# First layer of a four-layer transformer kernel: the spread of the head norms goes to the shifted scores' two PSUM banks, inside the MLP, and the splitting behind it among the last maxima

## The chip, the core and the metric

One core of a Trainium2 chip. The metric is device time in microseconds (us) of one execution, taken as the median of 3 runs. Of its engines the text uses these names: PE is TensorE (its matmuls), DVE is VectorE, ACT is ScalarE, POOL is GpSimd, SP is SyncE, which here issues nearly all DMAs of the main loop.

## What is computed

Four transformer layers over 32 sequences of 128 tokens with 144 features and 16 heads of 9 features. Layers 0 to 2 attend over the tokens, layer 3 over the heads of each token. The layers are alike but for this: only the first one normalises queries and keys per head. Cut from the reference:

```python
h = modulate(rmsnorm(x, g1, D), scale_msa, shift_msa)
qkv = h @ qkv_w.T + qkv_b
q = rmsnorm(q, qg, HEAD_DIM)          # layer 0 only
k = rmsnorm(k, kg, HEAD_DIM)          # layer 0 only
attn = softmax(einsum('bhqd,bhkd->bhqk', q * HEAD_DIM ** (-0.5), k))
o = einsum('bhqk,bhkd->bhqd', attn, v) @ proj_w.T + proj_b
x = x + gate_msa * o
h2 = modulate(rmsnorm(x, g2, D), scale_mlp, shift_mlp)
x = x + gate_mlp * (gelu(h2 @ fc1_w.T + fc1_b) @ fc2_w.T + fc2_b)
```

## The kernel before

The work is cut into 32 groups of 4 sequences: groups 0 to 7 are layer 0, 8 to 15 layer 1, and so on. Each engine runs its own written-out program, in order, and semaphores (`need(eng, name, g, k)`) tie them together. There is no scheduler: the order in the code is the order on the engine.

The main loop has one **body** per group g, from -1 to 31, and three groups are in work in it: g itself, J = g + 1 and L = g + 2.

- **Attention of g.** 16 steps. A step i multiplies keys and queries of 4 heads into one of two PSUM banks `st_bank` (`shifted_scores`, L1363), ACT takes the exponential out of it (L777), PE weights the values (L1383). The shift is the row maximum of each head, which is brought into the operand by small DMAs (`load_max`, L441, 2 DMAs for each of the 4 sequences b): step 0 needs sequence 0's (`m_loaded0`), step 4 needs `m_loaded1`, **step 8 needs `m_loaded2`** and step 12 `m_loaded3`.
- **In its gaps, the queries and keys of L** (L1283, L1287), in the other two banks, `score_bank`. In layer 0 DVE copies them out (`raw`), ACT squares them, PE sums them per head (L1295), ACT takes logarithm and exponential (`head_norms`, each with a table load), DVE refines the result (`newton`, its last line L1012).
- **Transition.** `o_to_tokens(g, 3)` (L1391), then in layer 0 `spread_norms(L)` (L1307): three matmuls T = 0, 1, 2 that copy each head's factor to its features, into `score_bank`; DVE multiplies (`fit`, L1021), ACT rounds to bf16 (`high`, L697), DVE takes the rest and rounds it (`mid`, L1030 and L1038), POOL takes what is left (`lows`, L563). PE goes on behind the spread with the values of J, first half (V0, L1317), the projection's second half, V1, and the MLP of g.
- **MLP of g** (`up` L1421, `down` L1447), first half, then second half, and among it the scores of J for their maxima (`scores`, L1338, steps 0 to 11; DVE `maximum`, L1052). At the end the maxima are turned by PE (L1347), copied by ACT (`copy_max`, L732) and loaded by DMA, upon which the next body's attention begins.

SP's order in a body is: maxima of g, sequences 2 and 3; store the 12 pieces of L's split queries and keys (`store_parts`, L390 and L384; 1.7 MB of writes); read them back, ordered for the scores, 4 DMAs of 512 KB (`load_stack`, L400); maxima of J, sequences 0 and 1; wait for g's last residual and load J's gates (L366, 2 DMAs of 288 KB). What is stored in body g for L is first used by `scores(L, 0)`, a body later.

Bodies 0 to 5 are those that have both g in work and a group L of layer 0 (groups 2 to 7).

Of the kernel before, what the change touches and what calls it, by code (L numbers as in the profile page):

```python
# [170 lines left out]
def blocks_kernel(nc, t, out):  # L171

    ctx = ExitStack()
    with ctx:  # L174
# [164 lines left out]
        def _(eng):  # L339
# [110 lines left out]
            def body(g):  # L450
                J, L = g + 1, g + 2
                if g >= 0 and flow_of(g) == "a":
                    load_max(g, 2)
                    load_max(g, 3)
                if J < NG and flow_of(J) == "t":
                    mix_values(J)
                if L < NG:
                    if L == FIRST_TOKEN_GROUP:
                        mask_on(L)
                    store_parts(L)  # L460
                    if L == 1:
                        eng.wait_ge(setup["split"], 7 * LAYERS)
                    load_stack(L)
                if J < NG and flow_of(J) == "a":
                    load_max(J, 0)
                    load_max(J, 1)

                if g < 0:
                    return
                need(eng, "x_mlp", g, 1)  # L470
                if layer_of(g) == LAYERS - 1:
                    at = first_seq(g)
                    eng.dma_start(out[at:at + GB].rearrange("b t d -> t b d"), x[:, at:at + GB, :])\
                       .then_inc(setup["out"], 16)
                if J < NG:
                    load_gates(J)
# [7 lines left out]
        def _(eng):  # L484
# [95 lines left out]
            def body(g):  # L580
# [13 lines left out]
                if L < NG and not layer_of(L):  # L594

                    lows(L)
                if g >= 0:
                    rstd_of(g, 1, 1)
                    add_mlp(g, 0)
                    add_mlp(g, 1)  # L600
# [6 lines left out]
        def _(eng):  # L607
# [196 lines left out]
            def body(g):  # L804
# [10 lines left out]
                if normed_heads:  # L815
                    high(L, 0)
                    high(L, 1)
                if g >= 0:
                    copy_oT(g, 3)
                if normed_heads:  # L820
                    high(L, 2)
                if g >= 0:
                    modulated(g, 1, 0)
                if late:
                    values(J, 1)
                if J < NG and not late:
                    mixed_values(J)
                for h in range(2 if g >= 0 else 0):
# [8 lines left out]
                    if h == 0:  # L837
                        modulated(g, 1, 1)
                if g >= 0:
                    first_use("exp_table", g, ACT.Exp)  # L840
# [9 lines left out]
        def _(eng):  # L850
# [165 lines left out]
            def fit(L):  # L1016

                for T in range(QKT):
                    need(eng, "spread_done", L, T)
                    need(eng, "qk_sq", L, T)  # L1020
                    eng.tensor_tensor(qk_raw[:, T, :], qk_raw[:, T, :], score_bank[T % 2][0:QKM, :], ALU.mult)\  # L1021
# [135 lines left out]
            def body(g):  # L1157
# [35 lines left out]
                if normed_heads:  # L1193
                    normalise(M, 0)
                    fit(L)
                    for T in range(QKT):
                        mid(L, T)
# [10 lines left out]
                if g >= 0:  # L1208
                    last_parts(g, 1, 1)
                    residual(g, 0, 1)  # L1210
                if J < NG:
                    for i in range(2, AHEAD):
                        maximum(J, i)
                        if i % CHUNKS == CHUNKS - 1:
                            split_max(J, i // CHUNKS)
                if g >= 0:
                    residual(g, 1, 1)
# [6 lines left out]
        def _(eng):  # L1224
# [41 lines left out]
            def queries_keys(L, T, long=True, short=True):  # L1266
# [5 lines left out]
                if long:  # L1272
# [3 lines left out]
                    if T < 2:  # L1276

                        need(eng, "max_done", L - 2, STEPS - 2 + T)
                        if L == 1:
                            need(eng, "qk_scaled", 0, QKT - 1)  # L1280
# [18 lines left out]
            def spread_norms(L):  # L1299

                need(eng, "norm_y", L, 0)
                for T in range(QKT):
                    if T == 0:
                        need(eng, "qk_taken", L, 2)
                    if T == 2:
                        need(eng, "qk_scaled", L, 0)
                    eng.matmul(score_bank[T % 2][0:QKM, :], spread[:, T * QKM:(T + 1) * QKM], norm_y[:, 1, :],  # L1307
# [13 lines left out]
            def scores(g, i):  # L1321
# [9 lines left out]
                elif g + 1 < NG:  # L1331

                    name = "qk_taken" if layer_of(g + 1) else "qk_scaled"
                    need(eng, name, g + 1, (2, 1)[i])
# [15 lines left out]
            def shifted_scores(g, i):  # L1350
# [8 lines left out]
                else:  # L1359
                    need(eng, "exp_done", g - 1, i - 2 + STEPS)  # L1360
                for j in range(CH):
# [144 lines left out]
            def body(g):  # L1506
# [6 lines left out]
                if L < NG and layer_of(L) == 0:  # L1513
# [25 lines left out]
                flip_rows(g, 1, 1)  # L1539
                down(g, 0)  # L1540
# [68 lines left out]
```

## Time and profile before

| what | value |
|---|---|
| median of 3 runs | 1935.79 us (1934.92 to 1936.99) |
| the profiled execution, its own time | 1931.41 us |
| its span | 1929.6 us |
| mean granted clock of TensorE | 0.875 of full speed |
| busy | PE 83%, DVE 66%, ACT 48%, POOL 20% of the span |

The profiled execution is 4.4 us shorter than the median. The granted clock has two levels in the rows below, 0.50 (1.2 GHz) and 1.00 (2.4 GHz), and a number between them where a window holds both. Times in rows are us from the start of the span. The first body with attention starts at 150.65 us; layer 0's bodies 0 to 5 fill 150.65 to 557.79 us.

### The profile page before, as it was taken

What the parts mean: (1) busy time and instruction counts of PE and PEld (TensorE: products, weight loads), DVE (VectorE), ACT (ScalarE), POOL (GpSimd) and SP (SyncE); (2) the same over time, 40 slices, a digit from 0 to 9 for tenths busy, and PEclk for the clock granted to TensorE, in tenths of its full rate; (3) what the DMA queues carried; (4) which work ended last, traced back from release to release, by engine and by line L of the source; (5) the groups of instructions that cost most, each with busy time, mean ns of one, the idle gap of its engine ahead of it and who ended that gap; (6) DMA issues with size and microseconds to landing.
All of it is one profiled execution on the core that took longest, in us unless ns stands there. A gap on an engine that the chain in (4) does not pass through costs nothing. (4 is left out here: it accounts for less than half of the span.)

```text
span 1929.6 us, 37580 instructions
## 1 busy us (share of the span) xinstructions
PE 1609.7 (83%) x13794; PEld 1045.1 (54%) x13794; DVE 1265.1 (66%) x3174; ACT 934.0 (48%) x2095; POOL 382.1 (20%) x432
## 2 busy tenths in 40 slices
PE   7357977977888999999898998989878777977888
PEld 4124544554455666666666666656555455555556
DVE  5664666576577767666767767676676677566743
ACT  0124445544555555555555556555444444443544
POOL 1020111011021111111111111111331434143310
PEclk9957777878899999998989989899788789787978
DMA  6150331232144433333333434343675777557530
GB/s 175 49 142 21 95 81 40 69 94 58 38 116 102 100 94 97 95 95 92 97 91 98 97 98 100 92 102 92 52 104 89 80 64 105 89 71 66 109 10 25
DMA packets 198009, 163.22 MB, mean 85 GB/s; under 512 B 80108, under 2 KB 182004, under 8 KB 191684
## 3 DMA queue, kind: packets, MB, share of 16 engines
q1 hardware_dynamic: 189444, 153.14, 40.7%
q10 hardware_dynamic: 8384, 7.69, 1.4%
q8 instruction: 111, 1.82, 0.4%
q14 instruction: 70, 0.57, 0.1%
HBM read 98.05 MB, written 61.95 MB: 83 GB/s over the span
## 5 line engine op out<-in xcount | busy, mean ns | idle before, releaser
L1052 DVE TENSOR_REDUCE maxima<-score_bank 128x4 f32<-128x512 f32 x512 | 339.3, 686 | 141.1 <-PE score_bank L1338 140.4
L777 ACT ACTIVATE p_room<-st_bank 128x512 f32<-128x512 f32 x512 | 299.4, 597 | 231.5 <-PE st_bank L1363 146.4
L1363 PE MATMUL st_bank<-stack_room 64*128 64x128 bf16 x2048 | 243.9, 234 | 43.6 <-DMA stack_room<-max_T 25.6
L1363 PEld LDWEIGHTS st_bank<-stack_room 64*128 64x128 bf16 x2048 | 147.2, 101 | 203.2 <-issue 138.7
L1421 PE MATMUL lin<-h2T,w_h 128*128 128x256 f32 (+1 forms) x640 | 223.3, 444 | 30.6 <-ACT h2T L667 17.6
L835 ACT ACTIVATE gelu<-lin 128x256 f32<-128x256 f32 (+1 forms) x320 | 119.0, 382 | 264.2 <-PE lin L1421 264.2
L1338 PE MATMUL score_bank<-stack_room 62*128 62x128 bf16 x2048 | 201.7, 227 | 8.5 <-DVE maxima L1052 5.8
L563 POOL TENSOR_TENSOR part_low<-qk_rest,part_mid 96x512 bf16<-96x512 f32 x96 | 116.9, 1218 | 437.8 <-DVE part_mid L1038 437.8
L1447 PE MATMUL lin<-w_f,gelu 128*128 128x144 f32 (+1 forms) x1280 | 190.0, 296 | 0.0
L1074 DVE RECIPROCAL o_recip<-o_bank 128x16 f32<-128x16 f32 x128 | 32.8, 256 | 234.6 <-PE o_bank L1391 234.6
L549 POOL TENSOR_TENSOR rstd<-var,neg_half 128x2 f32<-128x2 f32 (+1 forms) x96 | 77.1, 803 | 534.3 <-DVE var L912 299.3
L1383 PE MATMUL o_bank<-p_room,v_room 128*32 128x128 f32 x4096 | 182.1, 301 | 0.0
L1338 PEld LDWEIGHTS score_bank<-stack_room 62*128 62x128 bf16 x2048 | 126.5, 99 | 88.7 <-issue 45.9
L1447 PEld LDWEIGHTS lin<-w_f,gelu 128*128 128x128 f32 (+1 forms) x1280 | 163.7, 190 | 11.3 <-ACT gelu L835 0.3
L555 POOL TENSOR_TENSOR x<-x,gated 128x288 f32<-128x288 f32 x64 | 50.7, 793 | 511.5 <-DVE gated L1095 511.5
L1421 PEld LDWEIGHTS lin<-h2T,w_h 128*128 128x128 f32 (+1 forms) x640 | 99.2, 192 | 83.3 <-ACT gelu L835 35.8
L1283 PE MATMUL score_bank<-h1T,w_h 128*96 128x512 f32 x192 | 133.5, 786 | 8.8 <-ACT h1T L667 6.7
L661 ACT ACTIVATE hT_last<-lin,mods_rem 112x128 f32<-112x128 f32 x192 | 77.4, 454 | 119.3 <-issue 84.1
L1383 PEld LDWEIGHTS o_bank<-p_room,v_room 128*32 128x32 f32 x4096 | 104.9, 116 | 33.1 <-issue 7.8
L571 POOL COPY stack_room<-norm_room 128x4096 bf16<-128x4096 bf16 x16 | 112.4, 7051 | 0.0
L1063 DVE CAST max_parts<-maxima 128x16 bf16<-128x16 f32 x128 | 109.4, 854 | 3.4
L732 ACT ACTIVATE max_T<-lin 32x128 bf16<-32x128 bf16 x128 | 34.3, 268 | 157.4 <-PE lin L1347 156.3
(194 smaller groups left out, 2719.1 us busy)
## 6 DMA issues: line engine op xcount, KB each, us to landing
stack_room<-stack_dram SPq DMA_DIRECT2D x96, 512.0 KB, 7.6
gates<-gates_dram SPq DMA_DIRECT2D x64, 288.0 KB, 4.3
stack_dram<-part_high SPq DMA_DIRECT2D x64, 288.0 KB, 3.1
norm_room<-stack_dram SPq DMA_DIRECT2D x32, 512.0 KB, 8.1
stack_dram<-part_mid SPq DMA_DIRECT2D x64, 192.0 KB, 2.6
stack_dram<-part_high SPq DMA_DIRECT2D x64, 144.0 KB, 3.2
stack_dram<-part_mid SPq DMA_DIRECT2D x64, 96.0 KB, 2.8
stack_dram<-part_low SPq DMA_DIRECT2D x64, 96.0 KB, 2.1
```

The source lines that it names most:

```text
L563: eng.tensor_tensor(part_low[:, T, :], qk_rest[:, T, :], part_mid[:, T, :], ALU.subtract)\
L571: eng.tensor_copy(stack[J % 2][s].rearrange("p (c m) -> p c m", m=TOK), stage[s].rearrange("p (m c) -> p c m", m=TOK)).then_inc(S["reorder ...
L777: eng.activation(probs[:, i % PBUFS, :], st_bank[i % 2][:, :], ACT.Exp, scale=float(HD) ** -0.5)\
L835: eng.activation(gelu[0:m, T, half], lin[LIN_BANK[f"F{h}{T}"]][0:m, 0:GT // 2], GELU[layer_of(g)]).then_inc(S["gelu_ready"], 1)
L1052: eng.tensor_reduce(maxima[:, b, CH * c:CH * c + CH], score_bank[i % 2][:, :].rearrange("p (h k) -> p h k", h=CH), AX_X, ALU.max)\
L1063: eng.tensor_copy(parts[:, :, 0, :], full).then_inc(S["max_high"], 1)
L1283: eng.matmul(bank, w_h[l][:, cols], h1T[L % 2][:, :], start=True, stop=False)
L1338: ins = eng.matmul(score_bank[i % 2][:, j * TOK:(j + 1) * TOK], score_columns(0, g, b, c, j, MAX_ROW), score_columns(1, g, b, c, j, MAX_RO ...
L1363: ins = eng.matmul(o, score_columns(1, g, b, c, j, HALF), score_columns(0, g, b, c, j, HALF), start=True, stop=flow_of(g) == "a")
L1383: ins = eng.matmul(o_bank[b % 2][32 * j:32 * j + 32, c * TOK:(c + 1) * TOK], v_aug[:, b, CH * c + j, :], probs[:, i % PBUFS, j * TOK:(j + ...
L1421: return eng.matmul(lin[LIN_BANK[f"F{h}{T}"]][0:FCM[T], 0:GT // 2], w[:, cols], act[:, tok], **flags)
L1447: ins = eng.matmul(o, gelu[0:k, T, b * TOK:(b + 1) * TOK], w_f2[l][0:k, T, :], start=T == 0, stop=T == FCT - 1)
```

## The change

In bodies 0 to 5 `spread_norms(L)` writes to the two `st_bank` instead of the two `score_bank`, and stands on PE behind the second half's transposition (`flip_rows(g, 1, 1)`), ahead of `down(g, 0)`. DVE's `fit(L)` stands behind the MLP's second `last_parts`, ACT's three `high(L, T)` behind the last gelu, DVE's `mid(L, T)` among the maxima 8, 9 and 10 of J, POOL's `lows(L)` between the two halves of the last residual. The scores of J no longer wait for the fit, the shifted scores do. On SP the maxima of J, sequences 0 and 1, are now ahead of L's store and load in these bodies. The prologue and body -1 keep their order, with the spread in the `st_bank` too.

```diff
@@ sync, body
+                first = g >= 0 and L < NG and layer_of(L) == 0
+                if first:
+                    load_max(J, 0)
+                    load_max(J, 1)
                 if L < NG:
...
                     load_stack(L)
-                if J < NG and flow_of(J) == "a":
+                if J < NG and flow_of(J) == "a" and not first:
                     load_max(J, 0)
                     load_max(J, 1)
@@ gpsimd, body
                 if g >= 0:
                     rstd_of(g, 1, 0)
-                if L < NG and not layer_of(L):
+                if g >= 0:
+                    rstd_of(g, 1, 1)
+                if L < NG and not layer_of(L) and g < 0:
                     lows(L)
                 if g >= 0:
-                    rstd_of(g, 1, 1)
                     add_mlp(g, 0)
+                if L < NG and not layer_of(L) and g >= 0:
+                    lows(L)
+                if g >= 0:
                     add_mlp(g, 1)
@@ scalar, body
                     if h == 0:
                         modulated(g, 1, 1)
+                    if h == 1 and normed_heads:
+                        for T in range(QKT):
+                            high(L, T)
@@ vector, fit
-                    eng.tensor_tensor(qk_raw[:, T, :], qk_raw[:, T, :], score_bank[T % 2][0:QKM, :], ALU.mult)\
+                    eng.tensor_tensor(qk_raw[:, T, :], qk_raw[:, T, :], st_bank[T % 2][0:QKM, :], ALU.mult)\
@@ vector, body
                     last_parts(g, 1, 1)
+                if g >= 0 and normed_heads:
+                    fit(L)
+                if g >= 0:
                     residual(g, 0, 1)
                 if J < NG:
                     for i in range(2, AHEAD):
                         maximum(J, i)
                         if i % CHUNKS == CHUNKS - 1:
                             split_max(J, i // CHUNKS)
+                        if g >= 0 and normed_heads and 8 <= i < 8 + QKT:
+                            mid(L, i - 8)
@@ tensor, spread_norms
-                    if T == 0:
-                        need(eng, "qk_taken", L, 2)
+                    if T < 2 <= L:
+                        need(eng, "exp_done", L - 2, STEPS - 2 + T)
...
                     if T == 2:
                         need(eng, "qk_scaled", L, 0)
@@ tensor, body
-                if L < NG and layer_of(L) == 0:
+                if g < 0:
                     spread_norms(L)
...
                 flip_rows(g, 1, 1)
+                if L < NG and layer_of(L) == 0:
+                    spread_norms(L)
                 down(g, 0)
```

**SP, from the load of L = 2 in body 0 to the maxima of group 1, sequences 2 and 3, in body 1, of before.** `stack_room<-stack_dram` is `load_stack(2)`; the four `max_T` rows behind it are group 1's sequences 0 and 1, the four behind the gates its sequences 2 and 3.

```order
L400 DMA stack_room<-stack_dram 64x4096 [waits st_done,parts_stored]
L400 DMA stack_room<-stack_dram 64x4096 x3
L441 DMA stack_room<-max_T 2x8x128 [waits stack_loaded,mT_copied]
L441 DMA stack_room<-max_T 2x8x128
L441 DMA stack_room<-max_T 2x8x128 [waits mT_copied]
L441 DMA stack_room<-max_T 2x8x128
L366 DMA gates<-gates_dram 128x576 [waits x_mlp]
L366 DMA gates<-gates_dram 128x576
L441 DMA stack_room<-max_T 2x8x128 [waits mT_copied]
L441 DMA stack_room<-max_T 2x8x128
```

**The same place of the changed kernel**, from the last rows of the store on; group 1's sequences 0 and 1 were issued ahead of the whole store.

```order
L384 DMA stack_dram<-part_low 96x512 [waits qk_low]
L384 DMA stack_dram<-part_low 48x512 x2
L384 DMA stack_dram<-part_low 96x512
L400 DMA stack_room<-stack_dram 64x4096 [waits st_done,parts_stored]
L400 DMA stack_room<-stack_dram 64x4096 x3
L366 DMA gates<-gates_dram 128x576 [waits x_mlp]
L366 DMA gates<-gates_dram 128x576
L441 DMA stack_room<-max_T 2x8x128 [waits mT_copied]
L441 DMA stack_room<-max_T 2x8x128
```

What moved: the store (it waits for `qk_low`, POOL's last piece) and the 2 MB load stood two maxima loads and the gates' wait ahead of sequence 2's maxima; now nothing but the gates stands between the load and them.

**PE in body 0 of before, around the spread**, from the last transposition of the attention output to V0.

```order
L1391 MATMUL o_bank<-ident,o_room 128x128 x3
L1307 MATMUL score_bank<-norm_room,spread 96x512 [waits qk_taken,norm_y]
L1307 MATMUL score_bank<-norm_room,spread 96x512
L1307 MATMUL score_bank<-norm_room,spread 96x512 [waits qk_scaled]
L1317 MATMUL lin<-w_h,h1T 128x144 [waits proj_gated]
```

**PE in body 0 of the changed kernel, around the spread**, from the MLP's second transposition to `down(0, 0)` (L1469 there).

```order
L1277 MATMUL lin<-ident,normed_last 112x128
L1325 MATMUL st_bank<-norm_room,spread 96x512 [waits exp_done,norm_y]
L1325 MATMUL st_bank<-norm_room,spread 96x512 [waits exp_done]
L1325 MATMUL st_bank<-norm_room,spread 96x512 [waits qk_scaled]
L1469 MATMUL lin<-w_f,gelu 128x144 [waits gelu_ready] x5
```

What moved: the three matmuls, some 35 rows later on PE; the third still waits for the first product of DVE's fit.

**DVE in body 0 of the changed kernel, the last maxima of group 1** (before, the four L1052 rows stood here with nothing between them).

```order
L1061 TENSOR_REDUCE maxima<-score_bank 128x4 [waits max_low,score_done]
L1039 TENSOR_TENSOR qk_rest<-norm_room,part_high 96x512 [waits qk_low,qk_high]
L1047 CAST part_mid<-qk_rest 96x512 [waits parts_stored,qk_rest]
L1061 TENSOR_REDUCE maxima<-score_bank 128x4 [waits score_done]
L1039 TENSOR_TENSOR qk_rest<-norm_room,part_high 96x512 [waits qk_high]
L1047 CAST part_mid<-qk_rest 96x512 [waits qk_rest]
L1072 CAST max_parts<-maxima 128x2x8 [waits mT_done,max_done]
```

What moved: a `mid` behind each of the maxima 8, 9 and 10.

## Rows read from the trace of the kernel before

**Rows 1.** The page's first line

```profile
span 1929.6 us, 37580 instructions
```

**Rows 2.** Timeline of PE, transition of body 0; start us, us, engine line op

```profile
180.86 0.66 PE L1391 MATMUL o_bank<-ident,o_room 128*128 128x128 f32 x4 [2.66 <-ACT o_room L742]
182.52 3.73 PE L1307 MATMUL score_bank<-norm_room,spread 32*96 32x512 f32 x4 [1.00 <-DVE norm_room L1012]
...
190.59 0.85 PE L1317 MATMUL lin<-w_h,h1T 128*128 128x144 f32 x2
...
198.62 0.84 PE L1317 MATMUL lin<-w_h,h1T 128*128 128x144 f32 x2 [1.03 <-DVE gated L1095]
...
207.28 1.49 PE L1447 MATMUL lin<-w_f,gelu 128*128 128x144 f32 x10
```

**Rows 3.** Timeline of DVE, transition and MLP of body 0

```profile
187.61 0.40 DVE L930 COPY normed_last<-normed 128x448 f32<-128x448 f32 x1
187.92 1.27 DVE L1021 TENSOR_TENSOR norm_room<-norm_room,score_bank 96x512 f32<-96x512 f32 x2
...
193.98 0.42 DVE L1038 CAST part_mid<-qk_rest 96x512 bf16<-96x512 f32 x1
...
196.93 1.27 DVE L1038 CAST part_mid<-qk_rest 96x512 bf16<-96x512 f32 x1
198.12 0.44 DVE L1095 TENSOR_TENSOR gated<-lin,gates 128x288 f32<-128x288 f32 x1
...
209.74 0.42 DVE L983 TENSOR_TENSOR h2T_rem<-h_rest,h2T_rem 16x256 bf16<-16x256 f32 x1
```

**Rows 4.** ACT: one line's durations (ns min/median/max); timeline row

```profile
L697 ACT ACTIVATE part_high<-norm_room x24: 612/617/632, 94.6 to 533.2; 96x512 bf16<-96x512 f32 x24
...
218.22 0.27 ACT L732 ACTIVATE max_T<-lin 32x128 bf16<-32x128 bf16 x1 [0.34 <-PE lin L1347]
```

**Rows 5.** Timeline of SP's queue, body -1 and end of body 0

```profile
129.38 2.22 SPq L390 DMA_DIRECT2D stack_dram<-part_high  x4
...
135.12 1.89 SPq L384 DMA_DIRECT2D stack_dram<-part_low  x4
138.43 2.37 SPq L400 DMA_DIRECT2D stack_room<-stack_dram  x4
141.70 2.79 SPq L441 DMA_DIRECT2D stack_room<-max_T  x4
...
218.51 3.40 SPq L441 DMA_DIRECT2D stack_room<-max_T  x4
222.97 0.83 SPq L366 DMA_DIRECT2D gates<-gates_dram  x2
```

**Rows 6.** Timeline of PE, steps 0 and 8 of several attentions

```profile
150.65 0.58 PE L1363 MATMUL st_bank<-stack_room 64*128 64x128 bf16 x4 [8.56 <-DMA stack_room<-max_T]
...
221.04 0.39 PE L1363 MATMUL st_bank<-stack_room 64*128 64x128 bf16 x4 [0.73 <-DMA stack_room<-max_T]
...
357.87 0.39 PE L1363 MATMUL st_bank<-stack_room 64*128 64x128 bf16 x4 [0.73 <-DMA stack_room<-max_T]
...
370.78 0.39 PE L1363 MATMUL st_bank<-stack_room 64*128 64x128 bf16 x4
...
557.79 0.39 PE L1363 MATMUL st_bank<-stack_room 64*128 64x128 bf16 x4 [0.74 <-DMA stack_room<-max_T]
...
567.50 0.39 PE L1363 MATMUL st_bank<-stack_room 64*128 64x128 bf16 x4
```

**Rows 7.** Windows: us, PE, PEld, DVE, ACT, POOL busy; PEclk, DMA share, GB/s

```profile
139.50:149.50 10.00, 1.72 (x11) 0.88 (x10) 2.63 (x6) 0.53 (x2) 0.00 (x0) 0.50 0.97 211
...
204.00:206.00 2.00, 2.00 (x6) 1.28 (x6) 1.10 (x4) 0.53 (x2) 0.00 (x0) 0.58 0.08 26
...
224.00:227.00 3.00, 3.00 (x35) 2.38 (x35) 1.76 (x4) 2.35 (x6) 0.00 (x0) 0.50 0.56 192
...
232.00:234.00 2.00, 2.00 (x22) 0.60 (x20) 0.00 (x0) 0.95 (x3) 0.00 (x0) 0.75 0.00 0
```

More of the change, by code:

```diff
@@ L814, in body @@
                     values(J, 0)
-                if normed_heads:
-                    high(L, 0)
-                    high(L, 1)
                 if g >= 0:
                     copy_oT(g, 3)
-                if normed_heads:
-                    high(L, 2)
-                if g >= 0:
                     modulated(g, 1, 0)
+                else:
+                    for T in range(QKT):
+                        high(L, T)
                 if late:
@@ L838, in body @@
                         modulated(g, 1, 1)
+                    if h == 1 and normed_heads:
+                        for T in range(QKT):
+                            high(L, T)
                 if g >= 0:
@@ L1194, in body @@
                     normalise(M, 0)
+                if normed_heads and g < 0:
                     fit(L)
@@ L1279, in queries_keys @@
                         if L == 1:
[L1280 removed]
+                            need(eng, ("qk_taken", "norm_max")[T], 0, (QKT - 1, 0)[T])
                     else:
@@ L1302, in spread_norms @@
                 for T in range(QKT):
-                    if T == 0:
-                        need(eng, "qk_taken", L, 2)
+                    if T < 2 <= L:
+                        need(eng, "exp_done", L - 2, STEPS - 2 + T)
+                    if T < 2 and L == 1:
+                        need(eng, "qk_scaled", 0, (2, 1)[T])
                     if T == 2:
                         need(eng, "qk_scaled", L, 0)
-                    eng.matmul(score_bank[T % 2][0:QKM, :], spread[:, T * QKM:(T + 1) * QKM], norm_y[:, 1, :],
+                    eng.matmul(st_bank[T % 2][0:QKM, :], spread[:, T * QKM:(T + 1) * QKM], norm_y[:, 1, :],
                                start=True, stop=True).then_inc(S["spread_done"], 1)
@@ L1331, in scores @@
                 elif g + 1 < NG:
-                    name = "qk_taken" if layer_of(g + 1) else "qk_scaled"
-                    need(eng, name, g + 1, (2, 1)[i])
+                    if i == 1 and layer_of(g + 1) == 0:
+                        need(eng, "norm_max", g + 1, 0)
+                    else:
+                        need(eng, "qk_taken", g + 1, (2, 1)[i])
                 else:
@@ L1360, in shifted_scores @@
                     need(eng, "exp_done", g - 1, i - 2 + STEPS)
+                    if g + 1 < NG and layer_of(g + 1) == 0:
+                        need(eng, "qk_scaled", g + 1, (2, 1)[i])
                 for j in range(CH):
```

## Prediction

> **What bounds the kernel now.** The span [rows 1] was read first, then one body of layer 0 on each engine in order of time, then the DMA queue. No engine is the bound in these bodies: it is a chain that runs through PE, and its longest hole is the transition. In body 0 PE ends its last transposition at 180.86 + 0.66 = 181.52 us, spends the time from 182.52 on the spread, in which it waits for DVE, and reaches V0 at 190.59 and V1 at 198.62 [rows 2]. The reader should see that V0, V1 and all behind them do not need the spread: they stand behind it in PE's order, and the second residual (L1095 at 198.12) stands behind fit and mid in DVE's order [rows 3]. The second thing to see is the start of an attention: step 0 comes when sequence 0's maxima have landed. At the end of body 0 SP issues them at 218.51 [rows 5] and PE goes on at 221.04 [rows 6], 2.5 us later. In body -1, where the same DMAs are issued at 141.70, right behind the stack load of 138.43 [rows 5], PE waits 8.56 us for them, until 150.65 [rows 6], with the DMA engines at a share of 0.97 and 211 GB/s until 149.5 [rows 7]: small transfers that are issued behind the 2.1 MB load land behind it.
>
> **What the change takes away.** Without spread, fit and mid in the transition, V0 of body 0 starts at about 182.9, when the first residual is gated. V1 needs the second residual. DVE reaches it when it has normalised group 3, 187.61 + 0.40 = 188.0 [rows 3]; PE should have the projection's second half done by about then. The product takes 0.44, so V1 starts at about 188.95, with a transposition just ahead of it. Before it was 198.62 [rows 2]: **-9.7 us**. The bound is PE's own way: V0 to V1 took 198.62 - 190.59 = 8.0 us with its waits for DVE and ACT [rows 2], which would put V1 at 190.9 and leave -7.7. The stores and POOL's lows leave this stretch too; nothing waited for them there.
>
> **What it puts into the MLP.** The three spread matmuls start where down(0, 0) stood, 207.28 [rows 2], on the old clock face. The row shows 3.73 us for four passes, two of T = 0 and two of T = 1, at the low clock [rows 2]; by then the clock has risen (0.58 in 204 to 206, so near 205.5) [rows 7], so I take half: 0.93 us each, T = 1 ends at 209.15. T = 2 waits for DVE's first product, which stands behind last_parts, 209.74 + 0.42 = 210.16 [rows 3], and takes 0.64 (the pair took 1.27) [rows 3]: 210.85. T = 2 ends at 211.8. **+4.5 us**; at the low clock it would be 5.6, and with fit entirely hidden 2.8. Behind it PE runs as before.
>
> **At the end of the MLP.** ACT does three highs of 0.62 ahead of the copy of the maxima, which waited 0.34 for PE before [rows 4]: 1.85 - 0.34 = **+1.5 us** for step 0 of the next attention. DVE gets three mids: a subtraction as long as the fit's product (0.64) and a cast of 0.42, or 1.27 beside POOL's lows [rows 3], 3.2 to 5.7 us in all. Part of it fills waits for scores, the rest makes the last maxima later; the body is 1.5 later by itself, and PE asks for the last maxima a little behind step 0. Bounds 1.5 and 3. POOL's lows end about 1.3 us after step 0. The sum of a transition is -9.7 + 4.5 + 1.5 = **-3.7 us**, six times (bodies 0 to 5): **-22 us**. The denser PE may find the high clock sooner than before, where it stayed low up to 205.5 [rows 7]; 1 us a body, **-6 us** (bounds 0 and -2 each).
>
> **What is late next: sequence 2's maxima.** The move that matters is on SP. The store of L waits for the last low, so it now falls on the start of the next attention, and in SP's order the load of L and the gates stand ahead of the maxima of sequences 2 and 3. From step 0 of the next attention (call it S; SP is through with sequences 0 and 1 at about S, as their four issues take 2.8 us [rows 5] and step 0 needs 2.5 from the first):
>
> - the store: high 2.2, mid about 1.9, low 1.9, and 1.4 from the last issue to the load (138.43 - 135.12 - 1.89) [rows 5]: the load is issued at S + 7.4;
> - from the load's issue to the landing of maxima behind it 150.65 - 138.43 = 12.2 us [rows 5, 6];
> - the gates between them: 0.58 MB, a share of 0.56 of 3 us [rows 7], 1.7 us if packed, 3 as seen; I take 2.0.
>
> Sequence 2's maxima land at **S + 21.6**. Step 8 needs them. It comes at 567.50 - 557.79 = 9.7 us behind step 0 in body 6, where the clock is high, and at 370.78 - 357.87 = 12.9 in body 3, where it is low [rows 6]; bodies 2, 4 and 5 run like 6, body 1 like 3. PE is in order, and DVE's divisions, L's queries and keys, the copies and the MLP all stand behind step 8, so nothing fills the wait. It is 11.9 us in four bodies and 8.7 in two, in bodies 1 to 6: **+65 us**. Body 0 is spared, since the load of body -1 keeps its place.
>
> After such a wait the clock is low: it was in body -1's (0.50 in 139.5 to 149.5), and in body 1, which is low from near its start, it rose only in 232 to 234 [rows 7]. Body 3 against body 6 prices it: 12.9 - 9.7 = 3.2 us. I take 2.5 a body, **+15 us**, since the part behind step 8 holds more waits that a slower PE doesn't lengthen (bounds 0 and 3.2).
>
> By the Trainium skill ("TensorE: Matmul & The Clock Gate", HAM oscillation), waits for DMA between bursts send the clock down, and the price is half of the low time; some 10 low us would be 5 us a body, 15 us more in all. The trace agrees that the clock falls, not with the half (3.2). The skill's "DMA: Bandwidth & Descriptors" (Specifications) gives a core 358 GB/s of HBM, by which 2.7 MB would pass in 7.5 us; then the wait would be about 4.5 us shorter, 27 us in all, and the kernel near 1961. The trace shows 211 GB/s for this load, and I go by it.
>
> **The sum.** -22 - 6 + 65 + 15 = +52 us. Against the profiled execution that is 1931.4 + 52 = 1983; its own time is 4.4 us under the median of the runs, to which the same 52 gives **1988 us**, 2.7% slower.
>
> **Rivals.**
> - *The small transfers overtake the load.* Then they land 2.5 us after their issue, which is at S + 7.4 + 2.4 + 0.8 = S + 10.6, so at S + 13.1: 3.4 us late in four bodies, in time in the others, 14 us in all, and 1935.8 - 28 + 14 = **1922**, faster. It decides as soon as the landing is before S + 14.4, where waits and gains are equal (six transitions give 28, and 4 x 4.7 + 2 x 1.4 takes 22 and some clock). For it: body -1's maxima were four small DMAs behind one load only, and steps there had other new waits. Against it: the 8.56 us wait, and DMA traffic that ends 1.1 us before PE goes on. Chance 0.10, and 0.03 that no wait shows at all (**1908**).
> - *The wait is there but the rest gives more.* Dense MLPs with the clock high throughout (-2 a body) and no lasting low clock behind step 8 (0 instead of 15), landing 2 us sooner (-12): 1988 - 6 - 15 - 12 = **1955**. Slower still. Chance 0.15.
> - *The new end becomes the bound.* Lows late beside DVE's mids, the store later by 2 us, the spread at the low clock (+1.1), mids at 1.27 each (+1.5): about 4.6 us a body more, **2015**. For it: DVE's 3.4 at worst; against it: POOL has nothing else there. Chance 0.15.
> - *Losses and gains cancel* within 0.2%: only with a landing near S + 14, chance 0.03.
> - The forecast itself, 1970 to 2005: 0.54.
>
> **The numbers.** 0.2%, 4 us, is about what a measurement of this kernel tells from no change. Faster: 0.10 + 0.03 = 0.13. Same 0.03. Slower 0.84. The range 1950 to 2018 takes in the second and third rival and leaves out the first, with 0.17 or so outside it.
>
> **What would show it.** Right: PE's step 8 in bodies 1 to 6 stands with a wait of 8 to 12 us for DMA stack_room<-max_T; SP issues the load 7 us behind step 0; V1 comes 7.4 us behind the last transposition (17.1 before); the spread takes 4.5 us from the transposition to down(g, 0); step 0 of bodies 1 to 6 has its 0.7 us wait still. Wrong: a step 8 without a wait for DMA, or step 0 later than the copy of the maxima explains. The likeliest error of size is the landing, which counts six times: 1 us of it is 6 us of the result.

## The result, and the profile after

The changed kernel takes **2025.93 us** (median of 4, 2018.13 to 2029.98) against 1936.39 (median of 4, 1934.92 to 1945.28) of the kernel before: ratio 1.0448, 95% interval 1.0401 to 1.0495, 4.5% slower. The profiled execution is one of 2029.98 us; its span stands against [rows 1]:

```profile
span 2028.2 us, 37586 instructions
...
core 0: 2028.2 us, clock 0.848
```

The direction was as predicted, and the largest part of the loss is at step 8, as predicted; but the loss was 90 us and not 52, outside the range. Five views show where it is.

**SP's queue, body 1** (start us, us), which answers to [rows 5]. Step 0 of this body is at 218.25.

```profile
218.50 2.35 SPq L390 DMA_DIRECT2D stack_dram<-part_high  x4
220.88 3.46 SPq L390 DMA_DIRECT2D stack_dram<-part_mid  x4
224.77 1.83 SPq L384 DMA_DIRECT2D stack_dram<-part_low  x4
227.97 2.42 SPq L400 DMA_DIRECT2D stack_room<-stack_dram  x4
230.44 1.41 SPq L366 DMA_DIRECT2D gates<-gates_dram  x2
231.89 2.71 SPq L441 DMA_DIRECT2D stack_room<-max_T  x4
```

**PE in the same body, step 8** (the second row), which answers to [rows 6]:

```profile
230.87 0.40 PE L1385 MATMUL st_bank<-stack_room 64*128 64x128 bf16 x4
...
241.84 0.61 PE L1385 MATMUL st_bank<-stack_room 64*128 64x128 bf16 x4 [10.00 <-DMA stack_room<-max_T]
```

The load is issued at S + 9.7 (S is step 0), the maxima land 13.9 us later, at S + 23.6. The middle of the store matters here: four issues of `part_mid` take 3.46 us, and the load waits 1.4 us behind the last low.

**PE, transition of body 0**, which answers to [rows 2]: last transposition, V0, V1.

```profile
181.04 0.66 PE L1413 MATMUL o_bank<-ident,o_room 128*128 128x128 f32 x4 [2.66 <-ACT o_room L751]
183.07 0.85 PE L1335 MATMUL lin<-w_h,h1T 128*128 128x144 f32 x2 [1.37 <-DVE gated L1104]
...
188.84 0.75 PE L1335 MATMUL lin<-w_h,h1T 128*128 128x144 f32 x2
```

V1 comes 7.1 us behind the last transposition, where it took 17.1.

**PE, MLP of body 1**: the spread, and `down(1, 0)` behind it. Below it windows of the same stretch (us, PE, PEld, DVE, ACT, POOL busy; PEclk, DMA share, GB/s).

```profile
276.34 1.95 PE L1325 MATMUL st_bank<-norm_room,spread 32*96 32x512 f32 x4
279.94 1.20 PE L1325 MATMUL st_bank<-norm_room,spread 32*96 32x512 f32 x2 [1.65 <-DVE norm_room L1030]
281.07 2.77 PE L1469 MATMUL lin<-w_f,gelu 128*128 128x144 f32 x10
```

```profile
276.00:278.00 2.00, 2.00 (x8) 0.71 (x6) 0.90 (x4) 1.49 (x4) 0.00 (x0) 1.00 0.00 0
278.00:280.00 2.00, 0.35 (x2) 0.06 (x1) 1.90 (x5) 0.01 (x1) 0.00 (x0) 1.00 0.00 0
280.00:306.00 26.00, 25.72 (x111) 17.82 (x111) 11.94 (x23) 6.32 (x14) 3.54 (x4) 0.52 0.00 1
...
202.00:206.00 4.00, 4.00 (x20) 3.53 (x21) 0.68 (x1) 0.00 (x0) 0.00 (x0) 0.57 0.00 0
```

The prediction had this stretch as 4.5 us and "behind it PE runs as before". The 4.5 is right (276.34 to 281.07 is 4.7). But behind it the granted clock is at its lower level for the whole rest of the MLP, with PE busy 25.72 of 26 us: the ten matmuls of `down` take 2.77 us, 1.49 in [rows 2]. Only about half of PE's matmuls there have 128 rows; nearly all others, the scores above all, have 62 to 65. In body 0 (last window) the clock dips behind the spread too, with PE busy throughout, but comes back within 4 us, as in bodies 2, 3 and 4. In bodies 1 and 5 it stays down for some 37 us and so into the next attention, to some 14 us behind its step 0: from 281 to 318 us it is 0.50, with PE busy for 36.2 of the 37.

**Engines at the end of the MLP of body 0**: ACT's highs, the table load (ACT_TABLE_LOAD) for the exponential, the copy of the maxima; SP; step 0.

```profile
212.47 1.66 ACT L706 ACTIVATE part_high<-norm_room 96x512 bf16<-96x512 f32 x3
...
214.15 1.28 ACT L652 ACT_TABLE_LOAD   x1
...
215.55 0.25 ACT L741 ACTIVATE max_T<-lin 32x128 bf16<-32x128 bf16 x1
...
215.82 2.57 SPq L441 DMA_DIRECT2D stack_room<-max_T  x4
...
218.25 0.39 PE L1385 MATMUL st_bank<-stack_room 64*128 64x128 bf16 x4 [1.72 <-DMA stack_room<-max_T]
```

Cut into phases, both traces give this for bodies 0 to 6 (us; "last transposition" is its end; the last column is what the prediction's terms come to in that phase):

| phase | before | after | change, all bodies | predicted |
|---|---|---|---|---|
| step 0 to step 8 | 9.7 (4 bodies), 12.9 to 13.1 (3) | 12.8 in body 0, 22.7 to 24.6 behind it | +76.5 | +65 |
| step 8 to the last transposition | 18.0 to 18.4 (12.2 in body 6) | 18.0 in body 0, 20.7 to 21.9 behind it (14.0 in body 6) | +17 | +15 |
| last transposition to `down(g, 0)` | 23.4 to 25.8 (11.1 in body 6) | 18.0 to 18.5 (20.2 in body 0, 11.1 in body 6) | -37 | -37 |
| `down(g, 0)` to the next step 0 | 13.7 to 13.8 | 16.3 to 16.4 in four bodies, 23.1 to 23.2 in bodies 1 and 5 (13.7 in body 6) | +29 | +9 |

The sum is +86 of the 98.6 us between the spans. The other 12 are in bodies 24 to 31, which are layer 3, whose code did not change. There the same matmuls are busy for 12 us more, at a lower mean granted clock; before and after:

```profile
1430.95:1929.60 498.65, 398.50 (x3673) 269.05 (x3672) 313.93 (x659) 220.79 (x501) 151.97 (x98) 0.83 0.58 70
...
1517.51:2028.20 510.69, 410.18 (x3673) 274.99 (x3672) 313.22 (x659) 220.78 (x501) 151.94 (x98) 0.81 0.57 69
```

Experiment 7 comes back to this.

### The profile page after: what moved, and what is told of

Its sections match the earlier page's. It is cut to its first block and busy times, and to the rows that moved or that the text cites. A ratio compares the mean times of both kernels' runs of the same rounds, so it can differ in the third digit from the quotient of the medians.

```text
span 2028.2 us, 37586 instructions
## 1 busy us (share of the span) xinstructions
PE 1663.5 (82%) x13794; PEld 1081.6 (53%) x13794; DVE 1259.3 (62%) x3174; ACT 932.8 (46%) x2095; POOL 377.6 (19%) x432
## 5 line engine op out<-in xcount | busy, mean ns | idle before, releaser
L1385 PE MATMUL st_bank<-stack_room 64*128 64x128 bf16 x2048 | 255.0, 242 | 94.2 <-DMA stack_room<-max_T 84.3
L1385 PEld LDWEIGHTS st_bank<-stack_room 64*128 64x128 bf16 x2048 | 154.5, 105 | 266.4 <-issue 150.1
L1358 PE MATMUL score_bank<-stack_room 62*128 62x128 bf16 x2048 | 209.0, 233 | 10.3 <-DVE maxima L1061 7.8
L1469 PE MATMUL lin<-w_f,gelu 128*128 128x144 f32 (+1 forms) x1280 | 205.7, 312 | 0.0
L567 POOL TENSOR_TENSOR part_low<-qk_rest,part_mid 96x512 bf16<-96x512 f32 x96 | 112.4, 1170 | 469.4 <-DVE part_mid L1047 469.4
L1405 PE MATMUL o_bank<-p_room,v_room 128*32 128x128 f32 x4096 | 190.3, 311 | 0.0
L1469 PEld LDWEIGHTS lin<-w_f,gelu 128*128 128x128 f32 (+1 forms) x1280 | 177.7, 203 | 16.3 <-issue 6.0
L1358 PEld LDWEIGHTS score_bank<-stack_room 62*128 62x128 bf16 x2048 | 131.0, 101 | 96.7 <-issue 47.1
L1298 PE MATMUL score_bank<-h1T,w_h 128*96 128x512 f32 x192 | 145.9, 853 | 8.9 <-ACT h1T L676 6.7
L1413 PE MATMUL o_bank<-ident,o_room 128*128 128x128 f32 x512 | 90.6, 304 | 25.0 <-ACT o_room L751 25.0
```

Of the source, the lines that this page charges most:

```text
L567: eng.tensor_tensor(part_low[:, T, :], qk_rest[:, T, :], part_mid[:, T, :], ALU.subtract)\
L1298: eng.matmul(bank, w_h[l][:, cols], h1T[L % 2][:, :], start=True, stop=False)
L1358: ins = eng.matmul(score_bank[i % 2][:, j * TOK:(j + 1) * TOK], score_columns(0, g, b, c, j, MAX_ROW), score_columns(1, g, b, c, j, MAX_RO ...
L1385: ins = eng.matmul(o, score_columns(1, g, b, c, j, HALF), score_columns(0, g, b, c, j, HALF), start=True, stop=flow_of(g) == "a")
L1405: ins = eng.matmul(o_bank[b % 2][32 * j:32 * j + 32, c * TOK:(c + 1) * TOK], v_aug[:, b, CH * c + j, :], probs[:, i % PBUFS, j * TOK:(j + ...
L1469: ins = eng.matmul(o, gelu[0:k, T, b * TOK:(b + 1) * TOK], w_f2[l][0:k, T, :], start=T == 0, stop=T == FCT - 1)
```

## The experiments

Each ratio is to runs of the kernel before on the same chip, in brackets its 95% interval. Where experiments of different times or chips are compared, the ratios are the better measure, since the median of the kernel before moved between 1930 and 1936 us. What is said of single bodies comes from one profiled execution of each kernel.

**1. Only SP's order undone.** In bodies 1 to 6 the store and load of the group are issued a body later, behind the maxima of sequences 2 and 3:

```diff
                 load_max(g, 2), load_max(g, 3)
+                if g >= 1 and layer_of(g + 1) == 0:
+                    store_parts(g + 1)
+                    load_stack(g + 1)
...
-                if L < NG:
+                if L < NG and not first:
```

> The changed kernel, but on SP the store and the load of L are issued in the next body, behind the maxima of its sequences 2 and 3. Queue theory (the maxima of sequence 2 land late because the 2 MB load and the store stand ahead of them): step 8 comes at S + 9.7 or 13 again as before the change, without a wait for DMA, and the 9 to 10 us waits go. What is left are the transitions: 5.9 us less from the last transposition to down(g, 0), 2.6 us more from there to the next step 0, 3.3 us less in all, six times 20: 1916 us, or about 1930 if two MLPs run at the low clock as they did in the changed kernel. Rival (late parts: DVE's mids and POOL's lows at the end of the MLP hold the next body up): step 8 still late, above 1990 us.

Measured: 1982.44 us, ratio 1.0277 (1.0250 to 1.0305). The wait at step 8 is gone, steps 0 to 8 take 13.5 to 14.9 us, and the part behind them 18.0. So the wait is the queue's, as argued. But the time is at least 52 us over what was expected. `down(g, 0)` to the next step 0 takes 16.3 us in body 0 and 23.2 in each of bodies 1 to 5: the low clock behind the spread, now in five bodies and not in two. Each of these five stays down into the next attention. (Body 6 loses 8 us to the delayed store, see experiment 3.) So the wait at step 8 is only part of the loss, and another term was missing.

**2. The kernel before with SP's new order alone.** All other engines keep the order of before; SP has the maxima of J, sequences 0 and 1, ahead of the store and load.

> The kernel before, with SP's order alone taken from the changed one (maxima of J, sequences 0 and 1, ahead of the store and load of L in bodies 0 to 5); spread, fit, high, mid and lows stay in the transition. Queue theory: the parts are ready long before, yet the store begins only at S + 0.9, the load at S + 8 to 10, step 8 at S + 22 to 24 with waits of 9 to 11 us: six times 12.5, and 2.9 behind each for the low clock, 1936 + 92 = 2028 us. Its down(g, 0) to next step 0 stays 13.8. If the low clock of the MLP in two bodies comes from the long wait and not from the spread's, one or two of the MLPs are at 23 here too. Rival (late parts): no or short waits at step 8, 1936 to 1950 us.

Measured: 2036.57 us, ratio 1.0565 (1.0532 to 1.0598). PE's step 8 in body 1:

```profile
244.29 0.61 PE L1367 MATMUL st_bank<-stack_room 64*128 64x128 bf16 x4 [10.61 <-DMA stack_room<-max_T]
```

The waits at step 8 are 10.6 to 14.4 us, steps 0 to 8 take 23.3 to 24.2 and the part behind 19.1 to 22.0 in bodies 1 to 5. `down(g, 0)` to the next step 0 is 13.7 everywhere: SP's order alone gives the wait and the low clock behind it, and does nothing to the MLP. This was expected within 9 us (by the ratio, within 17).

**3. and 4. The third spread matmul behind `down(g, 0)`,** with SP's order of experiment 1 (first) and with that of the change (second):

```diff
                 flip_rows(g, 1, 1)
-                    spread_norms(L)
+                    spread_norms(L, (0, 1))
                 down(g, 0)
+                    spread_norms(L, (2,))
```

> As the run with the store behind the maxima, and PE's third spread matmul stands behind down(g, 0), so that PE never waits for DVE's fit in the MLP. Clock theory (the 1.65 us wait of the third spread sends the clock down inside the MLP): the clock stays at 1.00 from the spread to the next step 0, each body is 1.6 us shorter for the wait and 1 us or more for the clock, 1936 - 20 - 16 = 1900 us. DVE's fit then waits longer for the third spread and holds the first half's residual up by some 1 us, which PE meets only at the second half's second product. Rival (the clock falls for the work's density alone): a gain of the wait alone, 10 us against the first run.

> The changed kernel with its SP order, only the third spread matmul behind down(g, 0). Clock theory: the two bodies with 23.2 us from down(g, 0) to the next step 0 fall to 15 or so, the others by the 1 us of the dip; step 8 keeps its wait of 9 to 10 us: 2026 - 10 - 14 = about 2002 us. Rival (the low clock in these two MLPs comes down from the long wait at step 8): 23 us in some bodies still, about 2015 us.

Measured: 1928.62 us, ratio 0.9993 (0.9969 to 1.0016), and 1985.53, ratio 1.0288 (1.0254 to 1.0322). In both, no body shows 23 us behind `down(g, 0)`: it is 16.2 to 16.8, with the third matmul in it. The second run came out 17 us under the 2002 that were expected. Ten matmuls with 128 rows stand now where PE waited 1.65 us. With experiment 1 and the change itself this is a square:

| ratio to before | SP's order of the change | store behind the maxima |
|---|---|---|
| three spread matmuls in a row | 1.0448 | 1.0277 |
| third one behind `down` | 1.0288 | 0.9993 |

Two causes, each worth 1.6 to 3.0%, depending on whether the other is there, and with both mended the change neither gains nor loses. The first run was expected at 1900. ACT in its body 6 shows one part of what is missing:

```profile
556.59 0.59 ACT L709 ACTIVATE part_high<-score_bank 96x512 bf16<-96x512 f32 x1 [6.06 <-DMA stack_dram<-part_low]
```

The first high of group 8 overwrites what the delayed store of group 7 still reads. The rest is steps 0 to 8: 12.6 to 14.4 us in every body, where before four of the seven took 9.7.

**5. and 6. Two repairs on that version.** Group 7 keeps the old order on all engines (one group less is moved); and besides that, ACT's highs stand among the gelus of the MLP's second half, so that they no longer delay the copy of the maxima.

> The run with the third spread later and the store behind the maxima (1929 us), but body 5 (L = 7, the last group of layer 0) keeps the old order on all engines. In that run body 6 took 60 us against 46.7, because ACT's first high of group 8 waits 6 us for group 7's store. Theory: body 5 takes about 65 us, body 6 47 to 50 us: 1929 - 12 = 1917 us. Rival (body 6 slow for the low clock left over from body 5): 1925 or more.

> As the run before it, and ACT's three highs stand one behind each of the second half's first three gelus, where ACT waits 0.7 to 0.8 us for PE, instead of behind the last gelu. Theory: the copy of the maxima comes 1.5 us sooner in five bodies, and with the shorter hole ahead of step 0 (PE waits 1.7 us there) the clock stays up in some of the attentions (step 8 at S + 9.7 to 10 instead of 13 to 14): 1917 - 7.5 - 10 = about 1900 us; without the clock 1909. Rival (DVE's mids, not ACT, are what is late): no gain, 1917.

Measured: 1925.73 us, ratio 0.9979 (0.9944 to 1.0014), and 1926.33, ratio 0.9985 (0.9957 to 1.0013). Neither differs from experiment 3 beyond the noise; 1917 us and 1900 to 1909 us had been expected. The first repairs body 6 (60.1 to 46.7 us) and costs 3.2 in body 5. The second takes 1.1 us from the MLP's end and gives them back at once: steps 0 to 8 go from 13.2 to 14.3, since DVE, with the mids before it, is late with the last maxima. So the rival of its expectation held. Step 0 waits 0.75 us there, as little as before the change, and the attention starts at the low clock all the same. The row is PE's, two steps into the attention of body 2:

```profile
280.03 0.61 PE L1372 MATMUL score_bank<-stack_room 62*128 62x128 bf16 x4 [1.27 <-DVE maxima L1075]
```

**7. The kernel before once more.**

> The kernel before, once more, for its trace. The changed kernel lost 11.5 us in layer 3, whose code is the same. If that is the clock's own play, the bodies of layers 1 to 3 differ here from the first trace of before by some us too, with the clock low at other places; if it is a consequence of the change, they are the same to 1 us.

It took 1927.19 us. The first seven bodies of attention are 445.6 us long against 453.9 in the first profile, and in both profiles some bodies of layers 1 and 2 take 46.4 us and others 48.1 to 49.9, with the same program in each. So the kernel before already loses to a low clock at the start of some attentions, and which ones is not the same from run to run. Layer 3's bodies 24 to 31 take 504.2 us here against 498.7: nearly half of the 12 us that the change seemed to lose there comes with no change at all.

**8. and 9. What lets the clock fall in the MLP?** First guess: PE's 1.65 us of idling ahead of the third spread matmul. Two filler matmuls in that gap, on experiment 1's kernel, their result never used. In the first run they have the spread's own shape (32 rows in, 96x512 out, fp32):

```diff
                     if T == 2:
+                        for _ in range(2):
+                            eng.matmul(o_bank[0][0:QKM, :], spread[:, T * QKM:(T + 1) * QKM], norm_y[:, 1, :], ...)
                         need(eng, "qk_scaled", L, 0)
```

> The run with the store behind the maxima (1982 us, 23.2 us from down(g, 0) to the next step 0 in five of six bodies), with two more matmuls of the spread's shape on PE while the third waits for DVE's fit; they write to a bank of the attention output that nobody reads any more. Clock theory: PE has no hole before the third spread, the clock stays up through the MLP, 16.3 us instead of 23.2 in five bodies, and the attention behind it starts at 10 to 13 us for step 8 rather than 14.5: 1982 - 35 - 5 = about 1940 us, although nothing waits less. Rival (the order or the density of the work behind, not the hole, sets the clock): 1982 to 1986.

Measured: 1979.11 us, ratio 1.0291 (1.0225 to 1.0358), the same as without fillers (1.0277), with 23.2 us behind `down(g, 0)` in bodies 1 to 5. PE and windows of body 1:

```profile
260.56 1.95 PE L1333 MATMUL st_bank<-norm_room,spread 32*96 32x512 f32 x4
262.35 1.88 PE L1329 MATMUL o_bank<-norm_room,spread 32*96 32x512 f32 x4
264.16 2.01 PE L1333 MATMUL st_bank<-norm_room,spread 32*96 32x512 f32 x2
266.11 2.77 PE L1477 MATMUL lin<-w_f,gelu 128*128 128x144 f32 x10
```

```profile
263.00:264.00 1.00, 1.00 (x3) 0.16 (x1) 0.97 (x2) 0.00 (x0) 0.00 (x0) 1.00 0.00 0
264.00:265.00 1.00, 1.00 (x2) 0.39 (x2) 0.70 (x2) 0.00 (x0) 0.00 (x0) 0.60 0.00 0
265.00:266.00 1.00, 1.00 (x2) 0.00 (x0) 0.00 (x0) 0.00 (x0) 0.00 (x0) 0.50 0.00 0
266.00:289.00 23.00, 23.00 (x97) 16.33 (x96) 9.45 (x19) 5.23 (x11) 3.09 (x3) 0.50 0.01 1
```

PE is busy without a gap, and the clock falls all the same, in the middle of the spread. The theory of the idle gap fell here. What these matmuls have in common is that only 32 of PE's rows work (they are called thin below, and those with 128 rows full-height). So the second run takes 128 rows, with the same columns and type, and so the same time:

```diff
-    eng.matmul(o_bank[0][0:QKM, :], spread[:, T * QKM:(T + 1) * QKM], norm_y[:, 1, :], ...)
+    eng.matmul(o_bank[0][0:QKM, :], ident[:, 0:QKM], w_h[layer_of(L)][:, 0:512], ...)
```

> As the filler run (the SP order of the first experiment, two extra matmuls ahead of the third spread matmul), but the two extra matmuls take 128 rows instead of 32, with the same 512 columns, fp32 and so the same time (0.93 us each). Theory A, few rows at work for some 7 us on end let the clock fall in the MLP: with full-height matmuls in the middle the clock stays up in bodies 1 to 5, down(g, 0) to the next step 0 takes 16.3 us instead of 23.2, time near 1979 - 5 x 6.9 = 1945. Theory B, the clock falls by the place of the spread in the program or by what went before, whatever PE does there: 23.2 us again in bodies 1 to 5, time near 1979.

Measured: **1935.18 us**, ratio 1.0000 (0.9980 to 1.0019), 2.8% under the run above. Its body 1:

```profile
263.11 1.96 PE L1329 MATMUL o_bank<-w_h,ident 128*96 128x512 f32 x4
264.99 1.09 PE L1333 MATMUL st_bank<-norm_room,spread 32*96 32x512 f32 x2
266.02 1.49 PE L1477 MATMUL lin<-w_f,gelu 128*128 128x144 f32 x10
```

```profile
263.00:266.00 3.00, 3.00 (x7) 0.81 (x6) 2.27 (x5) 0.00 (x0) 0.00 (x0) 1.00 0.00 0
266.00:281.00 15.00, 13.06 (x100) 9.51 (x100) 11.40 (x21) 5.38 (x12) 3.09 (x3) 1.00 0.01 2
```

The clock stays at its upper level; `down(g, 0)` to the next step 0 is 14.8 to 15.5 us in bodies 0 to 5. Two full-height matmuls a body in place of thin ones are worth 44 us (by the ratios 56), because of what they keep the clock from doing. Between the two fillers the rows change, and with them the data; which of the two counts was not taken apart.

**10. The thin fillers without a wait.** On experiment 3's kernel (clock up), two 32-row fillers right behind the second spread matmul, `down(g, 0)` behind them.

> As the run with the SP order of the first experiment and the third spread matmul behind down(g, 0) (1928.6 us, the clock up in the MLP), but two extra 32-row matmuls of the spread's shape stand right behind the second spread matmul, so that 3.9 us of 32-row matmuls run on end ahead of down(g, 0) and 0.98 behind it. Theory A, the run of few-row matmuls lets the clock fall: some bodies show 23 us from down(g, 0) to the next step 0 instead of 16.3; with all five, 1928.6 + 1.9 x 6 + 5 x 6.9 = 1975. Theory B, the clock falls only where PE comes to T = 2 with the fit still open (a wait, or the fillers in it) just ahead of down: 16.3 in all bodies, 1928.6 + 6 x 1.9 = 1940.

Measured: 1961.43 us, ratio 1.0179 (1.0110 to 1.0248). Body 1:

```profile
258.73 1.95 PE L1328 MATMUL st_bank<-norm_room,spread 32*96 32x512 f32 x4
260.52 2.86 PE L1333 MATMUL o_bank<-norm_room,spread 32*96 32x512 f32 x4
263.31 2.77 PE L1477 MATMUL lin<-w_f,gelu 128*128 128x144 f32 x10
```

Bodies 1, 3 and 4 show 24.5 to 25.1 us behind `down(g, 0)`, bodies 0, 2 and 5 15.8 to 16.4. So nothing has to be waited for: four 32-row matmuls in a row, with `down` right behind, are enough in half the bodies. Adding thin work lowered the clock where there was no low clock before, which shows the cause from the other side. Why the other three bodies keep the clock is open, and full-height fillers were not run at this place.

**11. and 12. The same remedy at step 0.** There PE waits for sequence 0's maxima, 0.73 us before [rows 6] and 1.7 to 1.85 in the changed kernels. A full-height filler behind the last turning of the maxima fills this wait. (Thin fillers were not tried here, so these two runs don't tell whether the height counts or only that PE is busy.) First in experiment 5's kernel, but with the third spread matmul back ahead of `down(g, 0)` and experiment 9's two fillers ahead of it, then in the kernel before:

```diff
                 if J < NG:
                     flip_max(J, 1)
+                if J < NG and flow_of(J) == "a":
+                    filler(g, 2 if moved(g) else 1)
```

(`moved(g)` is true in bodies 0 to 4; in the kernel before it is one filler everywhere.)

> The changed kernel with the SP order of the first experiment, group 7 at its old place and two full-height fp32 matmuls ahead of the third spread matmul (as in the full-height run, 1935.2 us), and the same kind of matmuls behind the last turning of the maxima, where PE waits for sequence 0's maxima ahead of step 0: two in bodies 0 to 4 (1.86 us into a wait of 1.85), one elsewhere in layers 0 to 2 (0.93 us into 0.73). Theory A, a wait or thin work before step 0 lets the clock fall at the start of the attention: step 0 to step 8 takes 9.7 us in bodies 1 to 6 instead of 13.5, the lasting price of layer 0 goes, and the bodies of layers 1 and 2 all last some 46.6 us instead of alternating between 46.4 and 49.2: 1935 - 6 x 3.8 - 8 x 2.8 + 17 x 0.2, near 1893. Theory B, the thin matmuls of the attention itself let it fall: no change in 0 to 8, time near 1930.

> The kernel before with one full-height fp32 matmul (0.93 us) behind the last turning of the maxima in all bodies of layers 0 to 2, where PE waits 0.73 us for the maxima ahead of step 0. Theory A: steps 0 to 8 take 9.7 us everywhere, where some bodies show 11.6 to 13.1 now; about eleven bodies at 2.8 us less, 23 at 0.2 more: 26 us less, near 1906. Theory B: half the bodies keep their slow attention, and the filler costs 0.2 us each: 1932 + 5 = 1937.

Measured: **1899.55 us** (1884.80 to 1906.65), ratio **0.9835** (0.9799 to 0.9870), and 1922.55 us, ratio 0.9937 (0.9918 to 0.9955). Both beat the kernel before; the first one is the best version found. Its profiled execution, 1884.80 us, is the fastest of the four, so its bodies show it at its best. Its PE at step 0 of body 2, and layers 1 and 2 in one window, ahead of the same window of the kernel before:

```profile
275.09 1.96 PE L1333 MATMUL o_bank<-w_h,ident 128*96 128x512 f32 x4
277.03 0.39 PE L1407 MATMUL st_bank<-stack_room 64*128 64x128 bf16 x4
...
600.00:1300.00 700.00, 640.19 (x6137) 421.47 (x6135) 500.40 (x1399) 410.46 (x946) 119.77 (x181) 1.00 0.39 98
```

```profile
600.00:1300.00 700.00, 640.60 (x6013) 428.37 (x6012) 490.12 (x1368) 403.41 (x927) 118.12 (x178) 0.95 0.38 95
```

Bodies 8 to 22, of layers 1 and 2, now take 46.6 to 46.7 us each, with steps 0 to 8 at 9.7; in bodies 1 to 5 of layer 0 steps 0 to 8 take 10.6 and not 13.5. In the kernel before with a filler, bodies 7 to 22 gain 12 us (three of them still take 48.2 to 48.5) and bodies 0 to 6 gain 2.3, but layer 3's bodies 24 to 31, again without an edit, are 12 us longer than in the first profile; in this trace that is the larger part of the 17 us by which the time is over what was expected.

## Why the prediction was wrong, step by step

- **What is taken away in the transition: right.** V1 behind the last transposition 7.1 us (forecast 7.4).
- **The spread in the MLP, 4.5 us: right in itself** (4.7). **"Behind it PE runs as before" is the step that failed.** In body 0 the clock dips to 0.57 from 202 to 206 us; four bodies lose 1.5 us (16.3 less 13.76 less 1.1 for the copy, below), bodies 1 and 5 lose 8.3. That is 22.6 us for which the sum had nothing. (In bodies 2 and 6, behind the slow MLPs, step 0 has no wait left, so there the copy costs nothing and all of the 9.4 us is the clock's.) The rival with a spread at the low clock priced it at 1.1 us a body: it saw the three matmuls, not the 14 us of MLP behind them. Experiments 3, 8, 9 and 10 show that the thin matmuls of the spread bring the clock down. They don't show why it comes back within 4 us in four bodies and stays down for 37 in two with the same program. Where the spread stood before, PE waited for DVE and ACT anyway, and a low clock cost little.
- **The gain of 6 us for an earlier high clock: not contradicted.** The phase from the last transposition to `down(g, 0)` comes to -37 us, as the terms with this gain do. How much of it is the clock was not taken apart.
- **The highs ahead of the copy of the maxima, +1.5: right in kind, measured 1.1.** The copy now stands behind highs and table load and runs 1.16 us after PE is done, and step 0 waits 1.72 us in place of 0.73 (experiment 6 takes these 1.1 us away again). The table load, which was hidden in a wait for PE before, was not in the sum.
- **Sequence 2's maxima at step 8: right in mechanism, 12 us short in size.** Forecast: load at S + 7.4, landing at S + 21.6. Measured in body 1: S + 9.7 and S + 23.6; in bodies 1 to 6 the load is issued at S + 8.5 to 10.5. From the load's issue to the landing it is 13.6 to 14.2 us (forecast 14.2). The 2 us are the store. About half of them are `part_mid`'s issues, 2.5 to 3.5 us where 1.9 was taken, from a body in which they came after a pause (1.77 us there, 1.7 behind the highs). The rest is that the store begins 0.2 to 1.8 us behind S and has pauses. Step 8 then comes 2 us later than forecast on average, and six bodies of it make 12 of the 38 us by which the forecast was off. The rival in which small transfers overtake the load did not happen (experiment 2).
- **The low clock behind that wait, +15: right**, +17. The Trainium skill ("TensorE: Matmul & The Clock Gate", HAM oscillation) prices low time at half of it; by an estimate from that rule the figure would have been 30 in place of 15. The trace stands with the smaller one: bodies with the wait take 20.7 to 21.9 us for a part of 18.0 to 18.4. For the MLP behind the spread the price is nearer to the rule but below it: 23.2 us in place of the 14.9 of experiment 9, which is 8.3 us for 23.2 us of low clock.
- **Layer 3: 12 us that no term had.** Its bodies 24 to 31 take 498.7 us in the first profile, 504.2 in experiment 7, 497.2 in experiment 11 and 510.8 in experiment 12, with the same code. The longer ones have the lower mean clock, 0.81 against 0.83; what lowers it there is not explained.

The errors add up: 12 (steps 0 to 8, the late landing), 2 (the part behind), 23 (the clock in the MLP) less 2 (the copy), and 12 (layer 3) make 47; the span grew by 98.6 us where 52 was forecast. The late landing was the error that the prediction had named as the likeliest; the clock in the MLP is the larger one and was not in it.

Why did it not pay even with both causes mended (experiments 3, 5 and 6, ratios 0.998 to 0.999)? The transition does give 6 to 8 us a body (17.4 us in experiment 5, 23.1 to 25.4 in bodies 1 to 4 of the two traces of before). The third spread matmul and the late copy take 2.5 of it, and the clock takes the rest: in bodies 0 to 5 every attention starts low (13.2 us to step 8) where four of seven started high. The longer wait ahead of step 0 is an obvious suspect, but experiment 6 had it no longer than before, and its attentions started low too. In experiment 11, with full-height fillers at both places, the attentions start high and the moved spread shows its worth: in its one trace layer 0's bodies 1 to 4 take 62.0 to 63.6 us, against 64.9 in experiment 5 and 65.2 to 67.8 in the kernel before with its filler; by the medians it is 23 us ahead of that kernel.

## What to carry to other kernels

Before work is moved, ask what PE does around its new place: the kernel before hid thin 32-row matmuls in a stretch that waited anyway, and in a dense stretch the same matmuls let the clock fall and made 15 us of MLP work 23, in some bodies. A wait may be filled with matmuls of full height whose result is not used, and a run of thin matmuls broken up with them; here one such matmul a body took 0.6% off the kernel before, and the moved spread with fillers 1.7%. And a small transfer that PE needs in the middle of a stage must be issued ahead of the bulk transfer, not behind it: the queue's order cost 1.7 to 5.6% here, as much as or more than the stalls that the change removed.

## What the runs showed of the hardware that was not expected

- The granted clock fell with PE busy for the whole stretch: 1.00, then 0.60, then 0.50 in three consecutive microseconds of 32-row fp32 matmuls, and stayed at 0.50 for 23 us of gapless work behind it, half of its matmuls with 128 rows and half with 62 to 65 (experiment 8). The Trainium skill's "TensorE: Matmul & The Clock Gate" ties the fall to waits of PE, for DMA (HAM oscillation) or in short idles between groups of matmuls (A second HAM failure mode: psum-queue depth-cycling). Experiment 8 had no wait there, and experiment 9 held the clock with full-height matmuls of the same duration. What brings the clock back up again was not found.
- Issues on SP can get slower when they come together: the four of `part_mid` took 1.77 us in layer 0 of the kernel before, where 1.1 to 1.7 us lay between them and the highs, and 2.5 to 3.5 right behind the highs in the changed kernel. It is no general rule: the lows right behind the mids mostly took 1.8 to 1.9, in body 0 of before 3.18.
- A 2.1 MB load on SP's queue, with 0.58 MB of gates behind it, held back the small transfers issued behind both: in body 1 sequence 2's 4 KB transfers landed 13.9 us behind the load's issue, 10 us behind their own.
- With the same program, layer 3's bodies 24 to 31 took 497 to 511 us from kernel to kernel, against 498.7 in the first profile, at a mean granted clock of 0.83 to 0.81. No run here tells what lowers the clock there.
